# Routing of the last three quads at the seam between attention and expert steps: places and table of the sixth ahead, the seventh turned by PE, the eighth handled among the steps

## The reference, cut to what matters

```python
h = top_tokens(x)                                    # (32, 88, 192)
h = h + attn(layernorm(h))                           # 12 heads, fake-quantized, log-int softmax
xf = layernorm(h)
t = xf * rsqrt(mean(xf * xf) + 1e-5) * scale
g = t @ gate_w.T + gate_b                            # 16 logits for each of 2816 tokens
vals, idx = top_k(g, 4)
w = softmax(vals) / 4
u = einsum('th,ehf->tef', t, w1) + b1                # 192 -> 384
u = min(u_glu, 7) * sigmoid(1.702 * u_glu) * (clip(u_lin, -7, 7) + 1)
y = einsum('tei,eih->teh', u, w2) + b2
out = h + einsum('teh,te->th', y, full_w) * 4
```

## Time and profile before

| | |
|---|---|
| three runs | 656.61, 658.82, 659.18 us; median 658.82 |
| profiled execution | 656.87 us, of which its instructions span 655.1 us |
| granted PE clock, mean | 0.696 |
| busy, share of the span | PE 56%, DVE 82%, ACT 68%, POOL 62% |
| chain that ended last | PE 27%, DVE 23%, SP's queue 13%, issue 13%, DMA 12%, ACT 8%, POOL 2% |
| the attention's last softmax operation | until about 409 us |
| the first product of the steps | 429.2 us |
| the last scatter, the end | 618.1 us, 655.1 us |

### The profile page before, as it was taken

The page is one execution under the profiler, slowest core; times in us unless marked ns, Lnnn a source line. Parts: engine busy times, 40 slices in busy tenths (PEclk is TensorE's granted clock), DMA queues, the critical chain, the costliest instruction groups (busy, mean ns, idle before and its releaser), DMA issues.

```text
span 655.1 us, 13415 instructions
## 1 busy us (share of the span) xinstructions
PE 369.4 (56%) x3593; PEld 236.0 (36%) x3593; DVE 535.2 (82%) x1380; ACT 443.7 (68%) x782; POOL 402.9 (62%) x450
## 2 busy tenths in 40 slices
PE   0598254072452633534536221278979999999264
PEld 0144112031130311312313111256757777777153
DVE  3688699679898897798998989669769998988566
ACT  0046657478767677677686765376878899998753
POOL 9773433431546487586785885477777777777600
PEclk9999555555555555555555555578989999999679
DMA  8546997786959969743422432466467776682098
GB/s 196 67 64 179 366 279 154 257 250 209 304 124 335 226 205 324 154 102 85 114 53 61 101 73 64 107 147 135 116 142 141 124 136 137 137 143 60 14 390 306
DMA packets 191976, 107.76 MB, mean 164 GB/s; under 512 B 137746, under 2 KB 186011, under 8 KB 191906
## 3 DMA queue, kind: packets, MB, share of 16 engines
q1 hardware_dynamic: 181634, 89.22, 56.2%
q0 software_dynamic: 10272, 17.70, 8.8%
HBM read 23.61 MB, written 60.67 MB: 129 GB/s over the span
## 4 chain that ended last, share of the span: by engine, by line
PE 27%; DVE 23%; SPq 13%; issue 13%; DMA 12%; ACT 8%; POOL 2%; DVEq 0%; POOLq 0%; ACTq 0%
PE pS L1925 8%; DMA pTs<-S_p 5%; PE pP L1925 5%; SPq L523 5%; PE pX L1943 4%; DVE S_e L1497 3%; DVE negmx L1422 3%; PE pO L1943 3%; SPq L611 2%; DMA w2s<-expert_rows 2%; SPq L514 2%; PE pS L1666 2%; DMA arena<-in_x_dram 2%; PE pS L1668 2%; DMA bias_rows_hl<-bias_hl 2%
## 5 line engine op out<-in xcount | busy, mean ns | idle before, releaser
L836 POOL DMA_INDIRECT expert_rows<-stage,dest x118 | 124.0, 1051 | 37.3 <-issue 29.6
L765 POOL DMA_INDIRECT region<-rows,slots x60 | 73.7, 1228 | 23.5 <-issue 16.3
L758 POOL CAST arena<-arena 128x384 bf16<-128x384 int8 x42 | 27.0, 643 | 70.0 <-ACT arena L926 69.3
L1843 PE MATMUL pP<-WpT,oq 128*128 128x192 bf16 x72 | 15.9, 359 | 74.0 <-ACT oq L1025 69.2
L1710 PE MATMUL pX<-arena,WA 128*128 128x384 f16 x86 | 34.9, 509 | 39.1 <-ACT arena L926 28.2
L765 POOL DMA_INDIRECT region<-arena,slots x36 | 45.5, 1265 | 18.4 <-issue 11.2
L926 ACT ACTIVATE arena<-pX,qkB,qkA 128x384 int8<-128x384 f32 x43 | 28.4, 661 | 41.6 <-PE pX L1710 41.6
L664 POOL TENSOR_TENSOR w1s<-stage,w1s 128x768 f16<-128x768 f32 (+1 forms) x16 | 33.8, 2113 | 32.9 <-ACT w2s L912 32.3
L1856 PE MATMUL pO<-pTs,vq 88*32 88x96 bf16 (+1 forms) x576 | 12.5, 238 | 71.5 <-DMA pTs<-S_p 71.3
L1497 DVE SCALAR_TENSOR_TENSOR S_e<-S_sq,kf,S_pow 128x1056 f32<-128x1056 f32 x24 | 38.2, 1591 | 16.7 <-ACT S_sq L1039 16.6
L1011 ACT ACTIVATE S_g<-S_w,kf 128x1056 int16<-128x1056 uint16 x24 | 30.3, 1264 | 27.7 <-DVE S_w L1427 27.7
(11 more groups left out here) (428 smaller groups left out, 1434.6 us busy)
## 6 DMA issues: line engine op xcount, KB each, us to landing
region<-zrow SPq DMA_DIRECT2D x11, 3200.0 KB, 12.2
w1s<-expert_rows SPq DMA_DIRECT2D x16, 384.0 KB, 8.0
stage<-in_L_ffn_w_dram SPq DMA_DIRECT2D x16, 192.0 KB
stage<-in_L_ffn_w_dram SPq DMA_DIRECT2D x32, 96.0 KB
w2s<-expert_rows SPq DMA_DIRECT2D x8, 384.0 KB, 11.7
arena<-in_x_dram SPq DMA_DIRECT2D x4, 672.0 KB
expert_rows<-stage,dest POOLq DMA_INDIRECT x118
out_dram<-xsel SPq DMA_DIRECT2D x8, 198.0 KB
```

The costliest lines, as they stand in the source:

```text
L765: pool.indirect_dma_start(region_rows, bass.IndirectOffsetOnAxis(ap=slots[q % 3][:, i, m:m + 1], axis=0), rows[q % 3][:, i, :].bitcast(I16 ...
L836: pool.indirect_dma_start(y_dram, bass.IndirectOffsetOnAxis(ap=dest[(st - 7) % 8][:, j:j + 1], axis=0), ysb[b][:, j, :], None, bounds_chec ...
```

## The change

- Slot 23: DVE's `find_slots` of the sixth quad stands behind the softmax's second operation, ahead of the residual and the ratio. PE's `count_rows(0)` moves from slot 24 to 23.
- Seventh quad: in slot 24 PE turns its rows into two banks of PSUM (pS), DVE copies them out, ACT's tEr and PE's gate products follow in the same slot (before: DMAs, slot 25); its ranks are in slot 25 (before 26), POOL's sends as well. SP's `turn_by_load` of it is gone.
- `step_blocks` is cut in three, `count_blocks`, `sum_blocks`, `step_blocks`; on DVE the turned rows are copied between the first two, the chosen experts of the seventh stand ahead of the third, its places ahead of `step_table(0)`.
- The residual rows of the last two tiles are in a function of their own (`add_rows`), in slots 24 and 26.
- Last quad: ACT's root and the load of the Gelu table stand behind the first copy into tEb, `high_rows` behind step slot 2 (`ROWS_AT`), DVE's `low_tail` too; turning, gate, rank, count and spread are one slot later (3, 5, 6, 7, 8), POOL's sends two slots later (`SEND_AT` 9), `Y_APART` is 8.
- The exponentials of the first six quads move on ACT from slot 23 of the attention to step slot 61, where the other two are.

```diff
+        def gate_at(st):
+            return NQ - 2 if st == NT else quad_at(st, GATE) if st != NT + 1 else None
+        def rank_at(st):
+            return NQ - 2 if st == NT + 1 else quad_at(st, RANK) if st != NT + 2 else None
...
-        TURN_AT, GATE_AT, RANK_AT, COUNT_AT, SPREAD_AT, WORDS_AT, WEIGH_AT = 2, 4, 5, 6, 7, HEAD + 1, 20
+        ROWS_AT, TURN_AT, GATE_AT, RANK_AT, COUNT_AT, SPREAD_AT, SEND_AT, WORDS_AT, WEIGH_AT = 2, 3, 5, 6, 7, 8, 9, HEAD + 1, 20
...
-            turn_by_load(LASTQ - 1)
...
-                if 7 <= st < 7 + 3 * TOPK // 2:
-                    for n in (2 * (st - 7), 2 * (st - 7) + 1):
+                if SEND_AT <= st < SEND_AT + 3 * TOPK // 2:
+                    for n in (2 * (st - SEND_AT), 2 * (st - SEND_AT) + 1):
                         send_row(LASTQ, n)
...
-                if st == NT - 1:
-                    for e in range(TAILQ):
-                        exp_gates(e)
...
-            act.activation(tv[:, 11:12], fs[:, 0:1], ACT.Gelu_apprx_sigmoid)
-            high_rows(LASTQ)
-            act.wait_ge(s["tails_zeroed"], 2)
...
+                if st == 0:
+                    row_root(LASTQ)
+                    act.activation(tv[:, 11:12], fs[:, 0:1], ACT.Gelu_apprx_sigmoid)
+                    act.wait_ge(s["tails_zeroed"], 2)
+                if st == ROWS_AT:
+                    high_rows(LASTQ)
...
-                    for e in range(TAILQ, NQ):
+                    for e in range(NQ):
                         exp_gates(e)
...
+                if st == NT - 1:
+                    find_slots(HEADQ - 1)
...
+                if st == NT:
+                    add_rows(NT - 2)
+                if st == NT + 2:
+                    add_rows(NT - 1)
...
+                if st == NT:
+                    count_blocks(0)
+                    for half in range(2):
+                        evac_rT(TAILQ, half)
+                    sum_blocks(0)
...
+                if st == NT - 1:
+                    count_rows(0)
+                if st == NT + 1:
+                    spread_table(0)
...
+                if st == NT:
+                    for half in range(2):
+                        turn_rows(TAILQ, half)
```

More of the change, by code:

```diff
@@ L364, in fill_order @@
                     order += [(st, "v", 1)] if i == 2 else []
-                if quad_at(st, RANK) is not None:
-                    order += [("rank", quad_at(st, RANK))]
+                if rank_at(st) is not None:
+                    order += [("rank", rank_at(st))]
+                if st == NT:
+                    order += [("rows", NQ - 2, m) for m in range(2)]
                 if quad_at(st, TURN) is not None and quad_at(st, TURN) == NQ - 1:
@@ L370, in fill_order @@
                     order += [(st, "qk", 4)]
-                if quad_at(st, GATE) is not None:
-                    order += [("gate", quad_at(st, GATE))]
+                if gate_at(st) is not None:
+                    order += [("gate", gate_at(st))]
                 if nxt and i < 2:
```

73 lines of the change are left out of this document (43 added, 30 removed).

## The result

The changed kernel takes 660.9 us (median of 11 runs, 658.5 to 662.4) where the kernel before, run beside it, takes 658.2 (11 runs, 655.9 to 660.3). The medians are 2.7 us apart; the ratio, by which the runs are compared from here on, is 1.0037, interval 1.0019 to 1.0055: 2.4 us slower. The forecast was 661.0. The profiled execution took 660.02 us with a span of 657.9 (before 656.87 and 655.1).

What follows compares the result with a forecast made beforehand. Bounds: the handover behind the attention and a second slow place at POOL's scatters, PE, ACT and DVE nearly full elsewhere. y(0)'s -0.8 turns into +1.8 at te(16), plus 0.9 for exponentials: 2.7 us slower, 661.0, range 656.5 to 665.0.

Steps and rivals of the forecast that it cites:

- Table cast: DVE's cast of the first table in the handover: 420.6 against 422.14, 1.5 us sooner.
- part 1: DVE finds the sixth quad's places at the start of slot 23: cost nothing, gain nothing by itself.
- Landing of the loads: Time from SP's order of a step's load until its data is there, at steps 2 and 16 too: 3.0 us.
- The clock: PE at half clock in step 2 behind 2.8 us of idling; 1.0 us sooner if the clock held.
- From the last send to te(16): 1.88 us from POOL's last region send to SP's order of step 16, then landing: 1.8 us lost at te(16).
- Exponentials: Six more on ACT in step slot 61, directly ahead of y(56), without cover: all behind 0.9 us later.
- The loop behind te(16): The step loop there is PE-bound as before, so a shift passes unchanged to the end.
- Part 4: Six of eight exponentials move on ACT from slot 23 to step slot 61: 0.9 us lost.
- part 3: Last quad's work among the steps: last quad's rows 3.5 us later, step 16 ordered 5.1 later through POOL.
- Rival 1: Last quad's rows don't hold PE and DVE: y(0) 4.0 us sooner, whole 1.1 us faster, 657.1; chance 0.25.
- rival 2: POOL stands empty 3.0 us between y(0) and y(3), step 16 later still: 5.1 us slower, 663.4; chance 0.18.
- rival 3: Table not sooner: step 0 ordered at 423.1 as before, all behind 1.5 us later, 662.5; chance 0.12.

Runs made afterwards that it cites:

- second execution: The changed kernel itself profiled and run once more, nothing edited; ratio to before 1.0036, +2.4 us.
- exps_back: Changed kernel with six of the eight exponentials back in slot 23 of the attention; ratio to before 1.0002, +0.1 us.
- ahead_send9: rows_ahead with POOL's sends of the last quad at slot 9 instead of 7; ratio to before 1.0027, +1.8 us.
- send7: Changed kernel with POOL's sends of the last quad at slot 7 instead of 9, run twice; ratios to before 1.0039 and 1.0021.
- rows_first: Changed kernel with last quad's rows behind te(0), its turn to spread one slot sooner, sends still at slot 9; ratio to before 1.0050, +3.3 us.
- rows_ahead: Parts 1 and 2 alone: changed kernel with last quad's work and six exponentials at their old places; ratio to before 0.9985, -1.0 us.
- table_first: Changed kernel with DVE's places of the seventh quad behind the first table, not ahead of it; ratio to before 1.0025, +1.6 us.
- places_late: Changed kernel with DVE's places of the sixth quad back behind the attention's work of slot 23; ratio to before 1.0044, +2.9 us.

## Why the prediction was right

The forecast, +2.7 us, met the +2.4 of the runs. Its chain of waits is the one that the traces show; that the sum came so near is in part luck, since errors cancelled. By its steps:

- **Table cast** 420.6 forecast, 420.91 measured; step 0 ordered 421.6, measured 421.89. The 0.3 are within the 0.4 by which the last ratio came late (406.81 for 406.39), and 0.2 of that are part 1's instructions, which were put at nothing; counted from the last ratio the cast is right to 0.1. The sixth's sends ended at 416.6 and not near 414, without effect.
- **Landing of the loads**, taken as 3.0 between 2.8 and 3.16: mis-sized. From order to the end of ACT's wait it was 3.55 for step 0 and 3.75 for step 2 (426.85 to 430.60), above the upper end; 2.93 for step 16. The first product came at 426.20 instead of 425.2, so 3.0 and not 4.0 us sooner.
- **The clock**, 1.0 us charged for half clock at step 2: not in this execution, where the step's four products took 0.61 us at 434.49 behind 2.69 us of idling. It cancelled the landing's error, and y(0) came at 441.40 with 441.2 forecast: luck. In the second execution the term was there (1.06 us, y(0) 0.6 later).
- **Last quad's rows** forecast to end at 432.1, measured 433.05 (landing); low halves 433.9 for 432.95; PE idle 2.69 for 2.8; tEr's end at 439.2 for 439.0.
- **POOL**: last send's end forecast 479.9, measured 479.73. It was empty for 0.7 us in sum where 0.6 was charged.
- **From the last send to te(16)**: mis-sized. 2.82 us passed from its end to the order, not the 1.88 from 474.80 to 476.68 in the earlier trace rows: 0.8 of the difference are the send's late landing and 0.15 SP's slower way from there to the order. te(16) came 2.45 later than before, 2.0 counted from the last ratio, where 1.8 was forecast.
- **Exponentials** 0.9: from y(55) to POOL's last scatter 0.9 against before itself (14.0 for 13.1 us), 1.5 against exps_back, 1.4 on average over all kernels, 0.9 to 2.3 by the runs. The six activations were sized rightly (0.8 from the table load to y(56)); the slow scatter of y(56) was not foreseen.
- **The loop behind te(16)** was taken to pass a shift unchanged. It gave back 0.4 to 0.5 of it in the two executions of the changed kernel (te(16) to y(55) 121.5 and 121.6 us, before 122.0), which cancelled the errors at te(16) and in the tail in part.

So the sum was right to 0.3 us with five terms off by 0.4 to 1.0 each, which cancelled, and that nearness is luck: the landing, the way from the last send to te(16) and the exponentials were too small, the clock and the shift behind te(16) too large. The sign is no luck: parts 1 and 2 alone are 1.0 us faster than before and the whole is 2.4 slower. Part 4 costs about 1.5, which leaves about 1.9 for part 3; no run has part 3 alone. Part 3's cost goes through POOL to step 16, in two ways: by the order of its instructions (ahead_send9, send7) and, where the order is given back, by its wait for the last quad's later places (send7). Its own gain, the sooner first product, is lost within 15 us in the last quad's turn (rows_first had half of it back). Rival 1 is out (y(0) at 441.40, not 438); rival 2 did not happen here (y(3) 9.0 us behind y(0)), but appeared as described in two experiments, ahead_send9 and rows_first; rival 3 is out by the table's cast.

One thing said of part 3 was too strong: that POOL's order turns the gain into the whole loss. In the changed kernel itself, giving the order back brought 1.9 us at te(16), but 0.4 to 0.7 at the end. The last quad's being ready one slot later costs about as much there: te(16) of send7's two executions is 1.0 and 2.3 us behind that of rows_ahead, with the sends in the same slot.

## What to carry to other kernels

When work is put between the steps of a loop, its own time is the small part: ask for whom the next engine then queues, and count the instructions on the slowest queue (here POOL's, 0.97 us and 0.30 of gap each) between the loop's first result and the transfer on which a later stage waits. A free place for it is where an engine already waits for a load, as ACT did for 9 us; a place behind the loop's last full stretch, as slot 61, cost more here than its instructions (1.4 us for 0.8). And one profiled execution is not enough for terms of 1 us: count its stages from an instruction that the change doesn't touch, and look at a second execution.

## What was not expected of the hardware

- The same instruction stream had either clock level at the same place. In eight executions with a turn of the last quad behind te(2), the products of step 2 were at the lower clock in four, behind 1.94, 2.10, 2.25 and 2.81 us of idling, and at the full one in four, behind 1.46, 1.69, 2.44 and 2.69 us. Four products took 1.03 to 1.06 us or 0.60 to 0.61. y(0) came at 34.2 to 34.7 in the four at full clock, and at 35.2, 35.5 and 36.2 in three of the others (the fourth, table_first, had its table 0.8 sooner). The length of the last gap alone does not tell which it will be. The Trainium skill's page "TensorE: Matmul & The Clock Gate", in "Why this matters for your kernels", asks that PE have no long gaps between bursts. The gaps here are all shorter than those that it warns of, and four of the eight executions lost the clock all the same; so a gap that the page does not warn of can cost the clock, and the prediction's lower level behind 2.8 us could come out either way, as it did in the two executions of the changed kernel.
- A step's transposing load took 2.9 us from its order to ACT's going on at step 16, but 3.55 to 3.75 us in the first three steps of the same execution. In table_first and places_late it took 3.0 to 3.2 in all of the first three, and at step 16 of ahead_send9 and places_late 3.5. No run here tells what makes the difference.
- Two single transfers on POOL's queue were slow at the same place in one kernel after the other: a scatter of y(56) with 1.65 us for 0.97 wherever all eight exponentials stand in slot 61 (1.29 once), and the last region send, which landed up to 0.8 us late where an instruction packet fell on its end. Both are told above; neither cause was tested.
